# Four weight-load buffers instead of two, and two PSUM tiles for the scaling rows after attention

## The chip, the cores and the metric

The kernel runs on all eight cores of one Trainium2 chip. Each core computes one of the eight batch entries of x and has its own copy of all weights; the cores exchange nothing. The metric is the device time of the slowest core in microseconds (us). One execution of the program before was taken with the hardware profiler; the trace has all eight cores, and rows are of core 3, the slowest, where no other core is named.

## What is computed

One layer: a layer norm, differential attention with rotary embedding (two softmaxes, their weighted difference under a third softmax), a per-head RMS norm, the output projection, and beside it a feed-forward branch with Hadamard transforms, 8-bit activations and ternary weights. Cut to the lines that the two changed stages compute:

```python
def weight_quant(w):                    # for w_up and w_down
    scale = jnp.clip(jnp.mean(jnp.abs(w)), 1e-05, None)
    q = jnp.clip(jnp.round(w / scale), -1.0, 1.0) * scale
    return w + jax.lax.stop_gradient(q - w)
...
att = jnp.einsum('bhqv,bvhd->bqhd', diff, v)
att = att * jax.lax.rsqrt(jnp.mean(att * att, axis=-1, keepdims=True) + EPS) * rms_w
att = att * (1.0 - LAM_INIT)
return att.reshape(b, s, E) @ Wo
...
xn = _layernorm(x, axis=-1)
s = attention(xn)
g = _silu(hbitlinear(relu(hbitlinear(xn, w_up))**2, w_down))
x = x + s * g
```

## The kernel before

A core works through its stages one after the other: constants and the lambda row; the mean absolute value of both feed-forward weights (the weight-scale stage, from 14 us); layer norm; Hadamard transform and quantization of x; the projections to q, k and v with rotary embedding; attention (from about 2150 us); the scaling stage (5966 to 6213 us); the output projection; the two feed-forward products with a second Hadamard transform between them.

Each stage is a list of `Step`s, each with an engine, an amount by which it raises that engine's semaphore (its lane: sy for SyncE, te for TensorE, ve for VectorE, sc for ScalarE, gd for GpSimd), and an `after`: the steps it waits for. Without an `after`, a step waits for the step before it in the list. `Ch.run` (L84) emits the steps of each engine in the order of the list, inside one block, and a block ends with a barrier over all engines (the branches of L123 and L152 in the rows). A step waits at L136 until its predecessors' lanes have reached their counts. A step on SyncE or GpSimd for which another step waits also waits for its own transfer before its engine goes on (L151):

```python
if s.eng in ("sync", "gpsimd") and i in waited:
    eng.wait_ge(mysem, post[i][1])
```

So each of these two queues has at most one such transfer under way. SyncE (SP) and GpSimd (POOL) issue DMAs; VectorE is DVE, ScalarE is ACT, TensorE is PE in the rows.

The weight-scale stage (L269 to L320) goes over 64 tiles of 128 x 2048 f32 (1 MB each): 32 of the transposed up weight, 32 of the transposed down weight. Even tiles are loaded by SP, odd ones by POOL (L288), into `wst[i % 2]`, and DVE sums the absolute values of each tile into a column of `acc` (L294). The load of tile i waits for the sum of tile i-2, which is step 2 * (i - 2) + 1 of the list. Then a few small steps turn the columns into two scales.

The scaling stage (L1002 to L1026) multiplies the attention output `attT` (128 partitions, 16 heads of 2048 tokens side by side, bf16) by one factor for each head and token. The 64 rows of factors, 512 wide, lie on 64 partitions of `taub`. Each of 32 rounds brings two of them into the one-partition tile `taurow` by a 4 KB DMA on SP (L1011); then, for each of the two, an f32 matmul with a row of ones (`onr`) copies it to all partitions in the PSUM tile `psRp` (L1017, two passes of the array), and DVE multiplies a 128 x 512 piece of `attT` by it (L1022). `psRp` is another name of `psRo`; `psAt`, the PSUM tile of the attention product, is idle here. No step has an `after`, so each waits for the one before.

Of the kernel before, what the change touches and what calls it, by code (L numbers as in the profile page):

```python
# [8 lines left out]
F32 = mybir.dt.float32  # L9
# [5 lines left out]
T = 2048  # L15
# [140 lines left out]
def build_program(taps=(), upto=99):  # L156
# [29 lines left out]
    out = dt("out", [T, E], F32, "ExternalOutput")  # L186
# [13 lines left out]
    with st:  # L200
# [24 lines left out]
        onr = sbuf("onr", [1, 128], F32)  # L225
# [5 lines left out]
        with ExitStack() as ph:  # L231
            sb = lambda n, sh, ty: ph.enter_context(nc.sbuf_tensor(n, sh, ty))
# [11 lines left out]
            steps = [Step("sync", 16 * len(loads),  # L244
                          lambda e, inc, _l=loads: [inc(e.dma_start(out=d[:, :], in_=s[:, :]), 16)
                                                    for d, s in _l])]
# [22 lines left out]
        with ExitStack() as ph:  # L269
            sb = lambda n, sh, ty: ph.enter_context(nc.sbuf_tensor(n, sh, ty))  # L270
            pt = lambda n, sh: ph.enter_context(nc.psum_tensor(n, sh, F32))
            wst = [sb(f"wst{i}", [128, 2048], F32) for i in range(2)]
            acc = sb("acc", [128, 64], F32)
            ucol, dcol = sb("ucol", [128, 1], F32), sb("dcol", [128, 1], F32)
            rtmp = sb("rtmp", [1, 1], F32)
            pA, pC = pt("pA", [128, 1]), pt("pC", [128, 1])
            tiles = [(wupT, r, c) for r in range(16) for c in range(2)] + \
                    [(wdnT, r, 0) for r in range(32)]
            steps = []
            ld_idx = {}  # L280
    
            for i, (w, r, c) in enumerate(tiles):
                eng = "sync" if i % 2 == 0 else "gpsimd"
                prev_red = 2 * (i - 2) + 1 if i >= 2 else -1
                ld_idx[i] = len(steps)
                steps.append(Step(eng, 16,
                                  lambda e, inc, _w=w, _r=r, _c=c, _i=i:
                                  inc(e.dma_start(out=wst[_i % 2][:, :],  # L288
                                                  in_=_w[_r * 128:(_r + 1) * 128,
                                                         _c * 2048:(_c + 1) * 2048]), 16),  # L290
                                  after=[prev_red] if prev_red >= 0 else -1))
                steps.append(Step("vector", 1,
                                  lambda e, inc, _i=i:
                                  inc(e.reduce_sum(acc[:, _i:_i + 1], wst[_i % 2][:, :],  # L294
                                                   axis=AX, apply_absolute_value=True)),
                                  after=[ld_idx[i]]))
            for name, lo, hi, col, wsx, rws in [("u", 0, 32, ucol, wsu_s, rwsu),
                                                ("d", 32, 64, dcol, wsd_s, rwsd)]:
                steps += [
                    Step("vector", 1, lambda e, inc, _lo=lo, _hi=hi, _col=col:  # L300
                         inc(e.reduce_sum(_col[:, :], acc[:, _lo:_hi], axis=AX))),
                    Step("tensor", 1, lambda e, inc, _col=col:
                         inc(e.matmul(pA[0:1, :], onc[:, :], _col[:, :], start=True, stop=True))),
                    Step("vector", 1, lambda e, inc, _w=wsx:
                         inc(e.tensor_scalar(_w[:, :], pA[0:1, :], 1.0 / NW_ELEM, 1e-5,
                                             AO.mult, AO.max))),
                    Step("vector", 1, lambda e, inc, _w=wsx:
                         inc(e.reciprocal(rtmp[:, :], _w[:, :]))),
                    Step("tensor", 1, lambda e, inc:
                         inc(e.matmul(pC[:, :], onr[:, :], rtmp[:, :], start=True, stop=True))),  # L310
                    Step("scalar", 1, lambda e, inc, _r=rws:
                         inc(e.copy(out=_r[:, :], in_=pC[:, :]))),
                ]
            steps.append(Step("vector", 1, lambda e, inc: (
                vsync(e, e.tensor_mul(combo[:, :], wsu_s[:, :], wsu_s[:, :])),
                vsync(e, e.tensor_mul(combo[:, :], combo[:, :], wsd_s[:, :])),
                inc(e.tensor_scalar_mul(combo[:, :], combo[:, :], float(C0))))))
            ch.run(steps)
# [3 lines left out]
        with ExitStack() as ph:  # L322
            sb = lambda n, sh, ty: ph.enter_context(nc.sbuf_tensor(n, sh, ty))
# [12 lines left out]
            steps = []  # L336
# [10 lines left out]
            for tt in range(16):  # L347
                p = tt % 2
                i_ld = add1(Step("sync", 16, lambda e, inc, _tt=tt, _p=p:
                            inc(e.dma_start(out=xt[_p][:, :],  # L350
                                            in_=x[_tt * 128:(_tt + 1) * 128, :]), 16),
                            after=[pv_v2[p]]))
# [3 lines left out]
                            after=[i_ld, pv_v1[p]]))  # L356
# [6 lines left out]
                    after=[i_sq]))  # L363
# [4 lines left out]
                            after=[i_v1]))  # L368
# [6 lines left out]
                    after=[i_sr, pv_tpl[p]]))  # L375
                pv_v2[p] = i_v2
                i_c = -1
                for fp in range(8):
# [7 lines left out]
                        after=[i_v2, pv_c[fq]]))  # L386
# [3 lines left out]
                                   in_=psT[2 * _q + 1][:, :]))),  # L390
                        after=[i_t] + ([pv_st[p]] if fp == 0 else [])))
# [4 lines left out]
                                out=xnT_h.rearrange("p (f t) -> p f t", f=16)[  # L396
                                    :, :, _tt * 128:(_tt + 1) * 128],
                                in_=xstg[_p][:, :].rearrange("p (f c) -> p f c", f=16)), 16),
                            after=[i_c]))
# [5 lines left out]
        with ExitStack() as ph:  # L405
            sb = lambda n, sh, ty: ph.enter_context(nc.sbuf_tensor(n, sh, ty))
# [54 lines left out]
            steps = []  # L461
# [12 lines left out]
            for tc in range(4):  # L474
# [3 lines left out]
                for f in range(16):  # L478
# [3 lines left out]
                                                     in_=xnT_h[:, _f * T + _tc * 512:  # L482
                                                               _f * T + (_tc + 1) * 512]), 16),
                                     after=[pv_xl[r4]]))
                    i_mm = add2(Step("tensor", 1, lambda e, inc, _r=r4:
                                     inc(e.matmul(psH2[_r][:, :], h128b_s[:, :], xsl[_r][:, :],
                                                  start=True, stop=True)),
                                     after=[i_xl, pv_mm[r4]]))
# [3 lines left out]
                                     after=[i_mm] + ([pv_q[bk]] if f == 0 else [])))  # L492
# [3 lines left out]
                                 lambda e, inc, _base=base, _bk=bk:  # L496
                                 slot_store.__setitem__(_bk, butterflies(e, inc, _base, _bk)),
                                 after=[i_ev_last, pv_tree[bk]]))
                i_prev = i_bf
                for r in range(7):  # L500
                    p2 = 64 >> r
                    i_d = add2(Step("sync", 16, lambda e, inc, _p=p2, _bk=bk:
                                    inc(e.dma_start(out=ptmp[_bk][0:_p, :],
                                                    in_=mx[_bk][_p:2 * _p, :]), 16),
                                    after=[i_prev]))
# [3 lines left out]
                                       after=[i_d]))  # L509
# [4 lines left out]
                                   after=[i_prev]))  # L514
# [40 lines left out]
        with ExitStack() as ph:  # L555
# [22 lines left out]
            steps = []  # L578
# [137 lines left out]
        with ExitStack() as ph:  # L716
# [66 lines left out]
            for g in range(KVH):  # L783
                gp_ = g % 2
                for hl in range(4):
# [27 lines left out]
                    for qc in range(4):  # L813
# [192 lines left out]
                Step("vector", 1, lambda e, inc:  # L1006
                     inc(e.reciprocal(taub[0:64, :], taub[0:64, :]))),
            ]
            for sb8 in range(32):
                steps.append(Step("sync", 16, lambda e, inc, _s=sb8:  # L1010
                                  inc(e.dma_start(  # L1011
                                      out=taurow[0:1, :].rearrange("p (r c) -> p r c", r=2),
                                      in_=taub[2 * _s:2 * _s + 2, :]), 16)))
                for rr in range(2):
                    r = sb8 * 2 + rr
                    steps.append(Step("tensor", 1, lambda e, inc, _rr=rr:
                                      inc(e.matmul(psRp[:, :], onr[:, :],  # L1017
                                                   taurow[0:1, _rr * 512:(_rr + 1) * 512],
                                                   start=True, stop=True))))
                    h, qc = r // 4, r % 4  # L1020
                    steps.append(Step("vector", 1, lambda e, inc, _h=h, _qc=qc:
                                      inc(e.tensor_mul(  # L1022
                                          attT[:, _h * T + _qc * 512: _h * T + (_qc + 1) * 512],
                                          attT[:, _h * T + _qc * 512: _h * T + (_qc + 1) * 512],
                                          psRp[:, :]))))
            ch.run(steps)  # L1026
            if att_t is not None:
                ch.run([Step("gpsimd", 16, lambda e, inc:
# [454 lines left out]
```

How the kernel before makes its waits and increments, by code:

```python
                def body(eng, _e=ename):  # L125
                    for i, s in enumerate(steps):
                        if s.eng != _e:
                            continue
                        preds = _preds(i, s)
                        if preds:
                            tg = {}
                            for j in preds:
                                ln, c = post[j]
                                tg[ln] = max(tg.get(ln, 0), c)
                            for ln, c in tg.items():
                                eng.wait_ge(self.sems[ln], c)
                        else:
                            for ln, c in base.items():
                                if c > 0:
                                    eng.wait_ge(self.sems[ln], c)
                        mysem = self.sems[s._lane]
                        got = {"n": 0}
                        def inc(instr, k=1, _g=got, _s=mysem):
                            _g["n"] += k
                            return instr.then_inc(_s, k)
                        s.fn(eng, inc)
                        assert got["n"] == s.inc, \
                            f"step {i} ({s.eng}): declared inc {s.inc} != emitted {got['n']}"
                        if s.eng in ("sync", "gpsimd") and i in waited:
                            eng.wait_ge(mysem, post[i][1])
# [54 lines left out]
        def vsync(e, instr):  # L206
            instr.then_inc(vssem, 1)
            vs_n[0] += 1
            e.wait_ge(vssem, vs_n[0])
            return instr
```

## Time and profile before

| | us |
|---|---|
| timed runs, median of 2 | 9626.44 (9611.37 to 9641.5) |
| the profiled execution | 9568.67 |
| its span (slowest core, core 3) | 9567.1 |
| spans of all cores | 9525.7 to 9567.1 |
| weight-scale stage, loads and sums | 14.6 to 287 |
| scaling stage | 5966 to 6213 |

The span runs from the first to the last instruction of a core; the profiled execution's time is that of the whole run. Busy times of an engine leave out waits. A DMA issue is seen on its queue (SPq, or the POOL engine), and what its landing releases is the next instruction that used the tile. An idle time in brackets stands before the instruction, with what ended it.

### The profile page before, as it was taken

Reading aid. Unit: us, or ns where it says so; the run is one execution under the profiler, and the core shown is the slowest. Engines: PE = TensorE matmul, PEld = TensorE weight load, DVE = VectorE, ACT = ScalarE, POOL = GpSimd, SP = SyncE. Lnnn points to the kernel's source line nnn. Section 1 sums busy time; section 2 is a strip of 40 time slices with the busy share of each in tenths; the row PEclk is TensorE's granted clock in tenths of the full one; section 3 lists DMA queues with packets and bytes.
Section 4 is the critical chain, followed back from the end, with each engine's and each line's share of the span. In section 5 each row is a group of like instructions: output and inputs, shape, how many; then the busy total and the mean of one; then the engine's idle time right before and its main releaser. Section 6 shows DMA issues by size and latency. Waiting matters only on the chain. (4 is left out here: it accounts for less than half of the span.)

```text
span 9567.1 us, 61516 instructions; the slowest of 8 cores (9525.7 to 9567.1 us)
## 1 busy us (share of the span) xinstructions
PE 3498.9 (37%) x12334; PEld 1342.0 (14%) x12334; DVE 3218.8 (34%) x8586; ACT 2035.6 (21%) x5222; POOL 959.3 (10%) x1684
## 2 busy tenths in 40 slices
PE   0110256662222222222222223555677101014776
PEld 0000022220000000000000000122233101011222
DVE  5356223333333333333323333100111666672222
ACT  0310023333333333333333333000122100000111
POOL 0000444330000000000000000033011000001111
PEclk9999978885555555555555555577788555556778
DMA  6411443330000000000000000022332110102332
GB/s 234 147 34 37 79 75 77 75 59 21 15 19 16 16 17 17 21 15 15 15 21 15 15 15 10 2 34 34 128 104 88 36 30 25 36 18 66 89 86 77
DMA packets 622473, 462.03 MB, mean 48 GB/s; under 512 B 366329, under 2 KB 572394, under 8 KB 611362
## 3 DMA queue, kind: packets, MB, share of 16 engines
q1 hardware_dynamic: 437538, 269.24, 10.2%
q0 software_dynamic: 184576, 188.85, 8.8%
q8 instruction: 121, 1.98, 0.1%
q14 instruction: 238, 1.95, 0.1%
HBM read 350.52 MB, written 98.57 MB: 47 GB/s over the span
## 5 line engine op out<-in xcount | busy, mean ns | idle before, releaser
L925 PE MATMUL psT<-idn_s,Pb 128*128 128x128 bf16 x1024 | 267.8, 265 | 2027.1 <-DVE Pb L902 1897.2
L1378 PE MATMUL psD<-K,tsl 128*128 128x512 bf16 x2048 | 567.1, 446 | 87.2 <-DVE tsl L1355 87.1
L1132 PE MATMUL psU<-xqs,tsl 128*128 128x512 bf16 x2048 | 522.5, 423 | 177.4 <-DVE tsl L1122 177.4
L1055 POOL DMA_DIRECT2D wost<-wo x256 | 135.9, 602 | 4103.4 <-DVEq L123 4065.3
L891 ACT ACTIVATE Pf<-e0b 128x128 bf16<-128x128 bf16 (+15 forms) x256 | 284.0, 1109 | 855.8 <-DVE e0b L887 855.8
L687 PE MATMUL psP<-xns,wqst 128*128 128x512 bf16 x2048 | 445.7, 380 | 2.0 <-ACT vstg L663 0.3
L855 ACT ACTIVATE e0b<-psE 128x512 bf16<-128x512 f32 (+3 forms) x640 | 341.6, 534 | 409.5 <-DVE psE L850 254.3
L925 PEld LDWEIGHTS psT<-idn_s,Pb 128*128 128x128 bf16 x1024 | 107.2, 105 | 2284.6 <-issue 2271.5
L832 PE MATMUL psE<-kg,qh 128*128 128x512 bf16 (+3 forms) x640 | 326.0, 510 | 269.5 <-DMA qh<-qT_h 150.7
L963 PE MATMUL psAt<-PT,vg 128*128 128x512 bf16 x640 | 256.3, 578 | 361.9 <-DMA PT<-Pb 361.9
L701 DVE TENSOR_TENSOR m1b<-Xc,ctab 128x512 f32<-128x512 f32 x160 | 110.7, 692 | 795.0 <-ACT Xs L697 795.0
L848 DVE TENSOR_TENSOR psE<-psE,tri_s 128x128 f32<-128x128 f32 x256 | 76.5, 299 | 823.2 <-PE psE L836 823.2
L836 PE MATMUL psE<-kg,qh 128*128 128x512 bf16 (+3 forms) x640 | 341.5, 536 | 0.0
L858 ACT ACTIVATE e1b<-psE 128x512 bf16<-128x512 f32 (+3 forms) x640 | 339.3, 530 | 0.0
L1178 DVE TENSOR_TENSOR W2f<-W2f 128x256 f32<-128x256 f32 x640 | 218.1, 416 | 291.8 <-ACT W2f L1236 288.5
L1236 ACT COPY W2f<-psH 128x256 f32<-128x256 f32 x256 | 95.2, 373 | 1012.4 <-PE psH L1231 1000.1
L687 PE MATMUL psP<-xns,wkst 128*128 128x512 bf16 x512 | 121.0, 397 | 494.9 <-DMA wqst<-wq 494.9
L1265 PE MATMUL psR<-mrow,onr 1*128 1x256 f32 x16 | 9.5, 694 | 790.1 <-DVE betar L1260 790.1
L1132 PEld LDWEIGHTS psU<-xqs,tsl 128*128 128x128 bf16 x2048 | 215.6, 106 | 484.3 <-issue 294.5
L1378 PEld LDWEIGHTS psD<-K,tsl 128*128 128x128 bf16 x2048 | 224.0, 112 | 405.9 <-issue 245.0
L611 POOL DMA_DIRECT2D wqst<-wq x512 | 272.4, 987 | 14.0 <-issue 14.0
L934 ACT COPY PT<-psT 128x128 bf16<-128x128 bf16 x512 | 136.5, 267 | 599.6 <-PE psT L925 599.6
(179 smaller groups left out, 6289.0 us busy)
## 6 DMA issues: line engine op xcount, KB each, us to landing
xns<-xnT_h SPq DMA_DIRECT2D x256, 128.0 KB
wstg<-wupT SPq DMA_DIRECT2D x512, 64.0 KB
h_h<-h2b POOLq DMA_DIRECT2D x128, 256.0 KB, 2.3
W2f<-h_h SPq DMA_DIRECT2D x256, 128.0 KB
wst<-wdnT SPq DMA_DIRECT2D x512, 64.0 KB
PT<-Pb SPq DMA_TRANSPOSE x1152
wst<-wupT SPq DMA_DIRECT2D x16, 1024.0 KB
wst<-wupT POOLq DMA_DIRECT2D x16, 1024.0 KB, 5.5
```

The lines of the kernel that those rows point to most:

```text
L611: inc(e.dma_start(out=wqst[_p][:, (hl * 2 + c2) * 2048 + ec * 128: (hl * 2 + c2) * 2048 + (ec + 1) * 128], in_=wq[ec * 128:(ec + 1) * 128, ...
L687: mm = e.matmul(psP[_b][:, :], _w[:, _wc + ec * 128: _wc + (ec + 1) * 128], xns[_xp][:, ec * 512:(ec + 1) * 512], start=(ec == 0), stop=(e ...
L832: e.matmul(psE0[_b][:, 0:_cw], qh[_hp][:, _qt * 128:(_qt + 1) * 128], kg[_gp][:, _kc * 512:_kc * 512 + _cw], start=True, stop=True)
L836: inc(e.matmul(psE1[_b][:, 0:_cw], qh[_hp][:, T + _qt * 128: T + (_qt + 1) * 128], kg[_gp][:, T + _kc * 512: T + _kc * 512 + _cw], start=T ...
L855: e.activation(e0b[:, _p * T + _kc * 512: _p * T + _kc * 512 + _cw], psE0[_b][:, 0:_cw], AF.Exp, scale=ISQ, accum_out=A0[:, _p * 4 + _kc:_ ...
L858: inc(e.activation(e1b[:, _p * T + _kc * 512: _p * T + _kc * 512 + _cw], psE1[_b][:, 0:_cw], AF.Exp, scale=ISQ, accum_out=A1[:, _p * 4 + _ ...
L891: inc(e.activation(Pf[:, 0:_ks], e0b[:, _p * T: _p * T + _ks], AF.Exp, accum_out=SZ[:, _p:_p + 1]))
L925: inc(e.transpose(psT4[_tb][:, :], Pb[:, _sl * T + _kt * 128: _sl * T + (_kt + 1) * 128], idn_s[:, :])),
L963: mm = e.matmul(psAt[:, :], vg[_gp][:, kt * 128:(kt + 1) * 128], PT[:, _of + kt * 512: _of + (kt + 1) * 512], start=(kt == 0), stop=(kt == ...
L1132: mm = e.matmul(psU[_b][:, :], tsl[_p][:, ec * 128:(ec + 1) * 128], xqs[:, ec * T + _tc * 512: ec * T + (_tc + 1) * 512], start=(ec == 0), ...
L1178: last = e.tensor_sub(W[free[idx]][:, :], W[slot[i]][:, :], W[slot[j]][:, :])
L1378: mm = e.matmul(psD[_b][:, :], tsl2[_p][:, ec * 128:(ec + 1) * 128], K2[:, ec * T + _tc * 512: ec * T + (_tc + 1) * 512], start=(ec == 0), ...
```

## The change

In the weight-scale stage there are four buffers `wst` (their tiles are now called wstt) and tile i goes to buffer i % 4; its load waits for the sum of tile i-4. In the scaling stage each step has an explicit `after`. The two rows of a round go to two PSUM tiles, `psRp` and `psAt`. A matmul waits for its round's DMA and for the multiply that last read its tile; a multiply waits for its matmul; and the DMA of a round waits for the second matmul of the round before.

```diff
-            wst = [sb(f"wst{i}", [128, 2048], F32) for i in range(2)]
+            wst = [sb(f"wstt{i}", [128, 2048], F32) for i in range(4)]
...
-                prev_red = 2 * (i - 2) + 1 if i >= 2 else -1
+                prev_red = 2 * (i - 4) + 1 if i >= 4 else -1
...
-                                  inc(e.dma_start(out=wst[_i % 2][:, :],
+                                  inc(e.dma_start(out=wst[_i % 4][:, :],
...
-                                  inc(e.reduce_sum(acc[:, _i:_i + 1], wst[_i % 2][:, :],
+                                  inc(e.reduce_sum(acc[:, _i:_i + 1], wst[_i % 4][:, :],
...
+            ps45 = [psRp, psAt]
+            pv_mul = {0: -1, 1: -1}
+            pv_mm2 = [-1]
             for sb8 in range(32):
-                steps.append(Step("sync", 16, lambda e, inc, _s=sb8:
+                i_d = add45(Step("sync", 16, lambda e, inc, _s=sb8:
...
+                                 after=[pv_mm2[0]] if sb8 else [1]))
                 for rr in range(2):
                     r = sb8 * 2 + rr
-                    steps.append(Step("tensor", 1, lambda e, inc, _rr=rr:
-                                      inc(e.matmul(psRp[:, :], onr[:, :],
+                    i_mm = add45(Step("tensor", 1, lambda e, inc, _rr=rr:
+                                      inc(e.matmul(ps45[_rr][:, :], onr[:, :],
...
+                                      after=[i_d, pv_mul[rr]]))
...
+                                       after=[i_mm]))
+                    pv_mul[rr] = i_mul
+                pv_mm2[0] = i_mm
```

What SP issues at the start of the weight-scale stage, before the change (the number behind wst is the buffer, L_sy, L_ve, L_te and L_sc are the lanes waited for, and x15 stands for fifteen such issues):

```order
L245 DMA oh_s<-ohd 128x127
L123 UNCONDITIONAL_BRANCH [waits L_sy]
L152 UNCONDITIONAL_BRANCH [waits barrier_Pool_Activation_PE_DVE_SP_release]
L288 DMA wst0<-wupT 128x2048 [waits L_sy,L_ve,L_te,L_sc]
L288 DMA wst0<-wupT 128x2048 [waits L_sy,L_ve] x15
L288 DMA wst0<-wdnT 128x2048 [waits L_sy,L_ve] x16
```

The same place of SP after the change:

```order
L152 UNCONDITIONAL_BRANCH [waits barrier_Pool_Activation_PE_DVE_SP_release]
L288 DMA wstt0<-wupT 128x2048 [waits L_sy,L_ve,L_te,L_sc]
L288 DMA wstt2<-wupT 128x2048 [waits L_sy,L_ve,L_te,L_sc]
L288 DMA wstt0<-wupT 128x2048 [waits L_sy,L_ve]
L288 DMA wstt2<-wupT 128x2048 [waits L_sy,L_ve]
L288 DMA wstt0<-wupT 128x2048 [waits L_sy,L_ve]
```

SP now alternates between buffers 0 and 2 (POOL between 1 and 3). Every issue still waits for the own lane L_sy, that is for SP's load before it; the wait for DVE is for an older sum.

What stands on TensorE at the start of the scaling stage before the change (each row is a matmul of two passes):

```order
L152 UNCONDITIONAL_BRANCH [waits barrier_Pool_Activation_PE_DVE_SP_release]
L1017 MATMUL psRo<-taurow,onr 128x512 [waits L_sy]
L1017 MATMUL psRo<-taurow,onr 128x512 [waits L_ve]
L1017 MATMUL psRo<-taurow,onr 128x512 [waits L_sy]
L1017 MATMUL psRo<-taurow,onr 128x512 [waits L_ve]
```

And after the change:

```order
L152 UNCONDITIONAL_BRANCH [waits barrier_Pool_Activation_PE_DVE_SP_release]
L1026 MATMUL psRo<-taurow,onr 128x512 [waits L_sy]
L1026 MATMUL psAt<-taurow,onr 128x512 [waits L_sy]
L1026 MATMUL psRo<-taurow,onr 128x512 [waits L_sy,L_ve]
L1026 MATMUL psAt<-taurow,onr 128x512 [waits L_sy,L_ve]
```

The order of the matmuls is the same; the second of a round now has its own PSUM tile and waits for the DMA rather than for the multiply just before it. On SP the DMA of a round waits for TensorE's lane instead of VectorE's. Before:

```order
L983 DMA msb<-msrow 1x16x32 [waits L_sy,L_sc]
L123 UNCONDITIONAL_BRANCH [waits L_sy]
L152 UNCONDITIONAL_BRANCH [waits barrier_Pool_Activation_PE_DVE_SP_release]
L1011 DMA taurow<-taub 1x2x512 [waits L_ve]
L1011 DMA taurow<-taub 1x2x512 [waits L_sy,L_ve] x31
```

And after:

```order
L983 DMA msb<-msrow 1x16x32 [waits L_sy,L_sc]
L123 UNCONDITIONAL_BRANCH [waits L_sy]
L152 UNCONDITIONAL_BRANCH [waits barrier_Pool_Activation_PE_DVE_SP_release]
L1019 DMA taurow<-taub 1x2x512 [waits L_ve]
L1019 DMA taurow<-taub 1x2x512 [waits L_sy,L_te] x31
```

Nothing is added to or taken from any queue, and nothing changes its place in one.

## Rows read from the trace of the kernel before

**Rows 1.** The page: the span, and the chain that ended last, by engine.

```profile
span 9567.1 us, 61516 instructions; the slowest of 8 cores (9525.7 to 9567.1 us)
...
PE 6%; DVE 1%; ACT 1%; issue 1%; SPq 0%; DMA 0%; DVEq 0%; ACTq 0%; POOLq 0%; POOL 0%
```

**Rows 2.** Busy time by stretch: the two stages. Columns as in the first row.

```profile
core 3: us, PE busy (x) PEld busy (x) DVE busy (x) ACT busy (x) POOL busy (x), PEclk, DMA share, GB/s
14.00:285.00 271.00, 0.00 (x0) 0.00 (x0) 144.06 (x64) 0.14 (x1) 17.08 (x32) 1.00 0.73 248
5966.00:6215.00 249.00, 130.62 (x128) 31.72 (x128) 44.18 (x65) 0.00 (x0) 1.44 (x3) 0.50 0.00 1
```

**Rows 3.** One tile: SP's loads to wst, durations in ns, first and last start.

```profile
L288 SPq DMA_DIRECT2D wst<-wupT x16: 327/328/328, 14.6 to 138.4; - x16
...
L288 SPq DMA_DIRECT2D wst<-wdnT x16: 327/328/328, 147.6 to 274.6; - x16
```

**Rows 4.** SP's own waits, 14 to 290 us: total, times, longest.

```profile
SPq L151 <- DMA wst<-wdnT: 90.5, 16, 7.6
SPq L151 <- DMA wst<-wupT: 88.0, 16, 6.0
SPq L136 <- DVE acc L294: 73.0, 31, 2.4
```

**Rows 5.** In order of time, one turn of POOL's loop: start, length, what.

```profile
84.53 0.53 POOL L288 DMA_DIRECT2D wst<-wupT  x1 [8.02 <-DVE acc L294]
...
89.84 2.29 DVE L294 TENSOR_REDUCE acc<-wst 128x1 f32<-128x2048 f32 x1 [2.00 <-DMA wst<-wupT]
92.68 0.53 POOL L288 DMA_DIRECT2D wst<-wupT  x1 [7.62 <-DVE acc L294]
```

**Rows 6.** One line: SP's DMAs of the scaling stage.

```profile
L1011 SPq DMA_DIRECT2D taurow<-taub x32: 558/558/621, 5966.3 to 6204.9; - x32
```

**Rows 7.** In order of time: the first round of the scaling stage.

```profile
5966.30 46.78 SPq L1011 DMA_DIRECT2D taurow<-taub  x7
...
5968.15 2.04 PE L1017 MATMUL psRo<-taurow,onr 1*128 1x512 f32 x2 [10.17 <-DMA taurow<-taub]
5970.30 0.69 DVE L1022 TENSOR_TENSOR attT<-attT,psRo 128x512 bf16<-128x512 bf16 x1 [4.08 <-PE psRo L1017]
...
5971.14 2.04 PE L1017 MATMUL psRo<-taurow,onr 1*128 1x512 f32 x2 [0.94 <-DVE attT L1022]
5973.28 0.69 DVE L1022 TENSOR_TENSOR attT<-attT,psRo 128x512 bf16<-128x512 bf16 x1 [2.29 <-PE psRo L1017]
```

**Rows 8.** Busy time in 17 to 22.5 us: cores 3, 5 and 0.

```profile
17.00:22.50 5.50, 0.00 (x0) 0.00 (x0) 2.29 (x1) 0.00 (x0) 0.00 (x0) 1.00 0.89 326
...
17.00:22.50 5.50, 0.00 (x0) 0.00 (x0) 0.80 (x1) 0.00 (x0) 0.00 (x0) 1.00 0.95 237
...
17.00:22.50 5.50, 0.00 (x0) 0.00 (x0) 1.93 (x1) 0.00 (x0) 0.00 (x0) 1.00 1.01 264
```

**Rows 9.** Busy time and granted clock: bursts of bf16 (L1065) and f32 matmuls (L1231).

```profile
6214.00:6224.00 10.00, 0.05 (x1) 0.08 (x2) 0.00 (x0) 0.00 (x0) 8.05 (x16) 0.50 0.57 53
6224.00:6229.00 5.00, 5.00 (x14) 1.79 (x15) 0.00 (x0) 0.00 (x0) 0.00 (x0) 0.55 0.00 0
6229.00:6234.00 5.00, 5.00 (x25) 2.29 (x24) 0.00 (x0) 2.46 (x3) 0.56 (x1) 1.00 0.09 30
...
7431.00:7434.00 3.00, 2.94 (x7) 2.43 (x8) 0.00 (x0) 1.66 (x3) 0.00 (x0) 0.50 0.00 0
7437.00:7440.00 3.00, 3.00 (x15) 2.64 (x14) 0.00 (x0) 2.42 (x7) 0.00 (x0) 1.00 0.00 0
```

**Rows 10.** In order of time: the first two loads on core 0, then core 3.

```profile
14.88 43.84 SPq L288 DMA_DIRECT2D wst<-wupT  x6
15.43 0.68 POOL L288 DMA_DIRECT2D wst<-wupT  x1 [14.74 <-POOLq L123]
...
25.27 2.29 DVE L294 TENSOR_REDUCE acc<-wst 128x1 f32<-128x2048 f32 x1 [2.41 <-DMA wst<-wupT]
...
14.63 98.61 SPq L288 DMA_DIRECT2D wst<-wupT  x13
...
22.95 2.29 DVE L294 TENSOR_REDUCE acc<-wst 128x1 f32<-128x2048 f32 x1 [0.95 <-DMA wst<-wupT]
```

More of the change, by code:

```diff
@@ L1008, in build_program, with add45 @@
             ]
-            for sb8 in range(32):
-                steps.append(Step("sync", 16, lambda e, inc, _s=sb8:
-                                  inc(e.dma_start(
-                                      out=taurow[0:1, :].rearrange("p (r c) -> p r c", r=2),
-                                      in_=taub[2 * _s:2 * _s + 2, :]), 16)))
+            def add45(stp):
+                steps.append(stp)
+                return len(steps) - 1
+            ps45 = [psRp, psAt]
+            pv_mul = {0: -1, 1: -1}
@@ L1014, in build_program @@
+            pv_mm2 = [-1]
+            for sb8 in range(32):
+                i_d = add45(Step("sync", 16, lambda e, inc, _s=sb8:
+                                 inc(e.dma_start(
+                                     out=taurow[0:1, :].rearrange("p (r c) -> p r c", r=2),
+                                     in_=taub[2 * _s:2 * _s + 2, :]), 16),
+                                 after=[pv_mm2[0]] if sb8 else [1]))
                 for rr in range(2):
                     r = sb8 * 2 + rr
-                    steps.append(Step("tensor", 1, lambda e, inc, _rr=rr:
-                                      inc(e.matmul(psRp[:, :], onr[:, :],
+                    i_mm = add45(Step("tensor", 1, lambda e, inc, _rr=rr:
+                                      inc(e.matmul(ps45[_rr][:, :], onr[:, :],
@@ L1018, in build_program @@
                                                    taurow[0:1, _rr * 512:(_rr + 1) * 512],
-                                                   start=True, stop=True))))
+                                                   start=True, stop=True)),
+                                      after=[i_d, pv_mul[rr]]))
                     h, qc = r // 4, r % 4
[L1021 to L1025, printed above, removed]
+                    i_mul = add45(Step("vector", 1, lambda e, inc, _h=h, _qc=qc, _rr=rr:
+                                       inc(e.tensor_mul(
+                                           attT[:, _h * T + _qc * 512: _h * T + (_qc + 1) * 512],
+                                           attT[:, _h * T + _qc * 512: _h * T + (_qc + 1) * 512],
+                                           ps45[_rr][:, :])),
+                                       after=[i_mm]))
```

## The prediction, made before the changed kernel ran

> **What bounds the kernel now.** I read the page first. Its chain of waits ends in the last matmul stage and covers some 8% of the span [rows 1]; the change touches nothing there. So the question is what two early stages are worth, each closed off by a barrier on both sides, so that whatever they gain moves the end by the same amount. I then took the stretches of the two stages, the counts and first and last starts of their instructions, SP's own waits, and one turn of each loop in order of time.
>
> The weight-scale stage: in 14 to 285 us the core does nothing but load 64 tiles of 1 MB and sum them. DVE is busy 144 of 271 us, the DMA share is 0.73 at 248 GB/s [rows 2]. SP's 32 loads start from 14.6 to 274.6 us, so a turn of SP's loop (two tiles, since POOL loads the other) is 260.0/31 = 8.39 us [rows 3]. SP's waits split it: 88.0 + 90.5 us over 32 for its own transfer (5.58 us each) and 73.0 over 31 for the reduce (2.35) [rows 4]; with 0.33 for the issue that is 8.26, and the rest hand-over. The reader should see one thing here: the queue issues one load, waits for it (L151), and only then for the reduce, so that each queue has at most one load in flight. On POOL the turn is issue 84.53, reduce from 89.84 (5.31 later), its end 2.29 later, next issue at 92.68, 0.55 after that [rows 5].
>
> The scaling stage after attention: 32 rounds that hold one small DMA, two f32 matmuls and two DVE multiplies. In 5966 to 6215 us PE is busy 52%, DVE 18%, and nothing else runs [rows 2]. SP issues from 5966.3 to 6204.9: 238.6/31 = 7.70 us a round [rows 6]. A round in order of time, counted from its DMA issue at 5966.30: matmul at 1.85, 2.04 long; multiply at 4.00, 0.69 long; second matmul at 4.84 (0.94 idle before it, released by DVE); second multiply at 6.98, done at 7.67; next DMA at 7.70 [rows 7]. Everything stands on one string.
>
> **The change in the load stage.** With four buffers the load i waits for reduce i-4, not i-2. It does not put more loads in flight: L151 still holds each queue until its own load has landed. What goes is the 2.35 us for the reduce from SP's turn, and 2.29 from POOL's. What is late next is the landing itself. If it stayed as it is, SP's turn would be 5.58 + 0.33 + about 0.1 = 6.0 us and POOL's 5.31 + 0.55 = 5.9. But 2.10 MB in 6.0 us is 350 GB/s, against 248 now, so landings may stretch. Bounds from rows: at the present ratio of rate to DMA share, a full share would be 248/0.73 = 340 GB/s, 6.2 us a turn. The only stretch of before with both queues loading at once on all cores is the start: in 17 to 22.5 us core 3 moves 326 GB/s at share 0.89 and core 5 237 GB/s at 0.95 [rows 8], which would be 6.4 and 8.8 us a turn; core 0 moves 264, 7.9 us. These first windows hold the ramp of the first transfers, so I lean to the fast side and take 6.6 us (318 GB/s), nearest to core 3, the core of this profile. Gain 31 x (8.39 - 6.6) = 55 us; ends 31 x (8.39 - 6.0) = 74 and 31 x (8.39 - 7.9) = 15, core 5's figure being left to the rivals. DVE hides under it: two reduces are 4.57 us plus some 0.2 between. The buffers cost nothing else; they are freed with the stage. POOL's later DMAs keep their place.
>
> [...]
>
> **The change in the scaling stage.** The two rows now go to two PSUM tiles, each matmul waits only for the DMA and for the multiply of the round before on its own tile, and the DMA waits for the second matmul in place of the second multiply. All instructions stay (32 DMAs, 64 matmuls of two passes, 64 multiplies). The round becomes: DMA to first matmul 1.85; four passes of f32 in a row; hand-over from PE to SP, about 0.1 (PE to DVE is 0.11 in the rows); next DMA. The four passes: two end after 2.04, and the second starts some 0.99 after the first, so two more add between 1.71 (twice 0.427 x 2, from the f32 passes of half the width, 7 in 3.0 us at the same clock [rows 9]) and 2.04. I take 1.90, so 3.94 in all, and a round of 1.85 + 3.94 + 0.1 = 5.89. The first multiply (0.69) lies beside the second matmul, the second beside the next DMA: it starts about 0.1 after the second matmul and is done some 1 us before the next round's first matmul, so the new waits on DVE are met long before. Behind a waiting matmul nothing is queued but the other matmul of the round. Gain 31 x (7.70 - 5.89) + 1.0 for the last round, whose first multiply is now hidden, = 57 us; ends 52 (four full passes, hand-over 0.15) and 63 (3.75 and 0.05).
>
> **Sum.** 55 + 57 = 112 us. The profiled execution took 9568.7 us, its span 9567.1; it would become 9456. The timed runs' median, 9626.4, is 58 above it, for reasons no row shows; I carry the gain over unchanged: 9626 - 112 = 9514 us. That is 1.2%, while a measurement of this kernel can tell about 2% from no change; so the sum, even if exactly right, counts as "within 2%".
>
> **Rivals.**
> Memory-bound: the loads already run at what memory gives to eight cores, and landings stretch as fast as the wait for the reduce goes. For it: share 0.73 now, and core 5 and core 0 at share 0.95 or more with 237 and 264 GB/s at the start. Against it: core 3's 326 GB/s at the same time. It would give 0 to 20 us, say 10: 9626 - 10 - 57 = 9559.
>
> [...] In the new order bursts are 3.9 us and gaps 2.0. The clock rose in rows only within longer unbroken bursts: 0.50 just before 6224, 0.55 in the first 5 us of a burst and 1.00 after that; there 14 matmuls in 5 us become 25, and the f32 passes go from 7 to 15 in 3 us [rows 9]. [...] If it rose, the four passes would take about 2.0 us; over two thirds of the rounds that is 21 x 1.9 = 40 us more: 9474. [...]
>
> Slower: with both queues of all eight cores always loading, the transfers trip over each other, as in the first pair. On core 0 that pair's second load, issued at 15.43, was reduced only at 25.27, and the first one was issued at 14.88: 10.4 us for two tiles [rows 10]. If every turn took that, the stage would lose 31 x (10.4 - 8.39) = 62 us and eat the 57 of the other: 9631, slower than before. It decides from a turn of 8.39 + 57/31 = 10.2 us on. Against it: the turn fell to 8.39 once loads were staggered, and core 3's first pair needed 8.3 us (14.63 to 22.95), start-up included [rows 10].
>
> Not as said: the second PSUM tile is no real second place, or the DMA still waits for DVE. The order of instructions shows neither; it would leave the gain of loads, 9571.
>
> **How the numbers follow.** Forecast 0.58, memory-bound 0.20, clock rises 0.13, slower than before 0.04, not as said 0.05. The likeliest is 9514. The range takes in memory-bound (9559, with some 25 us of scatter, as the two timed runs lie 30 apart) and the clock (9474, less the 19 us by which the load stage could beat its term): 9455 to 9585. Faster by over 2% needs 193 us, that is the clock over all rounds (60), both terms at their good ends (74 + 63): 197; chance 0.04. Slower by over 2% needs a turn of 16 us: 0.01. Within 2%: 0.95.
>
> **What would show it.** Right: SP's 32 weight loads from 14.6 to about 14.6 + 31 x 6.6 = 219 us, SP's waits for the reduce near zero and those for its landing above 5.6 us each, share over 0.9, DVE idle still released by DMA; in the scaling stage a round of 5.9 us, PE's idle time before the first matmul about 2 us and before the second none, SP released by PE. All other stages keep their lengths. Wrong: a turn above 7.5 us (memory-bound), above 10.2 (slower); a granted clock over 0.50 after attention (clock); 0.9 us idle still before every second matmul (not as said); or a later stage that changes by over 10 us, for which I name no cause.

## The result

Over all runs the changed kernel took 9504.65 us (median of 11, 9455.8 to 9589.55) and the kernel before 9625.29 (median of 10, 9547.24 to 9658.55). The ratio is 0.9882 with a 95% interval of 0.9843 to 0.992, so the change takes off 77 to 151 us, 114 in the middle: it is faster, by less than 2%. The forecast was 112 us and a time of 9514. Ratios compare fast executions alone, since in some executions of five of the kernels here cores 0 to 3 or cores 4 to 7 show a lower granted clock and take over 1% longer, as in one of the kernel before: cores 0 to 3 took 9705.2 to 9765.2 us at 0.661 to 0.665, the others 9523.1 to 9573.0 us at 0.678 to 0.683.

The profiled execution of the changed kernel took 9536.69 us; its slowest core is now core 4. Core 3, the core of the rows of before, went from 9567.1 to 9464.1. The first line of the page of the changed kernel, against [rows 1]:

```profile
span 9534.6 us, 61584 instructions; the slowest of 8 cores (9443.3 to 9534.6 us)
```

From the view of all cores, spans and mean granted clock of three; the other five end between 9443.3 and 9473.1, so cores 4 and 5 stand apart, of which more in the last section:

```profile
core 3: 9464.1 us, clock 0.677
core 4: 9534.6 us, clock 0.677
core 5: 9499.9 us, clock 0.682
```

The load stage of the changed kernel on core 3: SP's loads with their first and last start, against [rows 3].

```profile
L288 SPq DMA_DIRECT2D wstt<-wupT x16: 327/328/331, 14.8 to 125.0; - x16
...
L288 SPq DMA_DIRECT2D wstt<-wdnT x16: 327/328/328, 132.4 to 241.2; - x16
```

SP's waits there, against [rows 4]:

```profile
SPq L151 <- DMA wstt<-wupT: 109.9, 16, 8.1
SPq L151 <- DMA wstt<-wdnT: 108.4, 16, 7.7
```

The wait for the reduce (73.0 us before) has no row any more. SP's turn is (241.2 - 14.8)/31 = 7.30 us, against 8.39. But the landing, 5.58 us of waiting a load before, is now (109.9 + 108.4)/32 = 6.82: of the 2.35 us of waiting that went, 1.24 came back as a longer landing. The busy times of the stage and of the scaling stage on core 3, against [rows 2]:

```profile
core 3: us, PE busy (x) PEld busy (x) DVE busy (x) ACT busy (x) POOL busy (x), PEclk, DMA share, GB/s
14.00:251.00 237.00, 0.02 (x1) 0.00 (x0) 143.91 (x63) 0.17 (x1) 17.09 (x32) 1.00 0.87 283
5919.00:6097.00 178.00, 115.90 (x124) 35.92 (x124) 42.20 (x62) 0.00 (x0) 0.00 (x0) 0.50 0.00 1
```

One round of the scaling stage in order of time, against [rows 7]:

```profile
5919.38 6.26 SPq L1019 DMA_DIRECT2D taurow<-taub  x2
...
5921.23 2.04 PE L1026 MATMUL psRo<-taurow,onr 1*128 1x512 f32 x2 [10.17 <-DMA taurow<-taub]
...
5923.06 1.91 PE L1026 MATMUL psAt<-taurow,onr 1*128 1x512 f32 x2
...
5923.37 0.69 DVE L1032 TENSOR_TENSOR attT<-attT,psRo 128x512 bf16<-128x512 bf16 x1 [4.08 <-PE psRo L1026]
5925.08 0.69 DVE L1032 TENSOR_TENSOR attT<-attT,psAt 128x512 bf16<-128x512 bf16 x1 [1.02 <-PE psAt L1026]
5926.94 0.49 PEld L1026 LDWEIGHTS psRo<-taurow,onr 1*128 1x128 f32 x2 [3.54 <-issue]
5926.97 2.04 PE L1026 MATMUL psRo<-taurow,onr 1*128 1x512 f32 x2 [2.00 <-DMA taurow<-taub]
```

The second matmul has no idle time before it, where it had 0.94 us; the four passes take from 5921.23 to 5924.97, 3.74 us; the next matmul waits 2.00 us for its DMA. From first to last DMA it is 5919.4 to 6097.3, so a round is 5.74 us against 7.70, and this was the same on all eight cores. On core 3 the stages gave 33.8 us (the last sum of the load stage ends at 253.4, not 287.2) and 61.8 (31 rounds of 1.96 and the shorter last round). That is 96 of its 103 us. The rest is scatter of the other stages: between the last sum and the first multiply of the scaling stage core 3 took 5683 us before and 5670 after, while the cores of the kernel before take 5651 to 5691 there; and behind the scaling stage it lost 6 us.

### The profile page after: what moved, and what is told of

Read it like the earlier page. It is cut to its first block and busy times, and to the rows that moved or that the text cites. A ratio compares the mean times of both kernels' runs of the same rounds, so it can differ in the third digit from the quotient of the medians.

```text
span 9534.6 us, 61584 instructions; the slowest of 8 cores (9443.3 to 9534.6 us)
## 1 busy us (share of the span) xinstructions
PE 3489.5 (37%) x12334; PEld 1348.3 (14%) x12334; DVE 3221.7 (34%) x8586; ACT 2036.2 (21%) x5222; POOL 961.6 (10%) x1684
## 5 line engine op out<-in xcount | busy, mean ns | idle before, releaser
L1244 PE MATMUL psH<-W2f,h128f_s 128*128 128x256 f32 x512 | 133.7, 430 | 359.4 <-DMA W2f<-h_h 359.4
```

## The experiments

All but two are told against the changed kernel; lines of each are those of core 3.

**The loads alone.** The first three hunks of the change, the scaling stage as before.

> Four load buffers, the scaling stage as before the change. Theory (the two gains are independent, each stage closed off by barriers): SP's turn in the load stage 7.3 to 7.4 us as in the changed kernel, so 33 to 39 us off the time; the scaling stage keeps its 7.70 us a round. Rival (the load stage only shifts the cores against each other and a later stage gives the gain back): the same turn, but the layer norm to attention stretch longer by 20 us or more, time within 10 us of before.

It took 9598.41 us against 9636.99 of before, ratio 0.9958 (0.9921 to 0.9994): 40 us, between 6 and 76. SP's turn was 7.11 to 7.25 us over the cores, a little under the expected 7.3, and the round 7.70. The interval of the time alone does not exclude the rival of a later stage that gives the gain back, but the stage lengths do: from the last sum to the scaling stage the cores took 5657 to 5696 us, before 5651 to 5691. Cores 2 and 3 did lose 46 to 49 us in one later stage, which comes back in the last section.

**The scaling stage alone.**

> Two load buffers as before, the scaling stage as changed. Theory: SP's turn in the load stage back at 8.4 to 8.7 us, a scaling round of 5.74 us as in the changed kernel, 62 us off the time. Rival (the scaling stage gains more because it is reached earlier, at another granted clock): a round clearly other than 5.74 us, or a granted clock over 0.50 in it.

9561.18 us, ratio 0.9925 (0.9885 to 0.9964): 72 us, between 35 and 111. The turn was 8.32 to 8.61 us, the round 5.74, the granted clock 0.50. That the two parts are independent is shown by the turn and the round: each part alone has the value of the whole change in its own stage and that of before in the other. The times agree, 40 + 72 = 112 against 114, but each is uncertain by over 30 us.

**More loads in flight.** This asks what holds the turn at 7.3 us: memory, or the one load for each queue.

```diff
-                        if s.eng in ("sync", "gpsimd") and i in waited:
+                        if s.eng in ("sync", "gpsimd") and i in waited and not s._lane.startswith("wl"):
...
-                                  after=[prev_red] if prev_red >= 0 else -1))
+                                  after=[prev_red] if prev_red >= 0 else -1,
+                                  lane=f"wl{i % 4}"))
```

> As the changed kernel, but each of the four load buffers has its own semaphore and the queues no longer wait for their own load before they issue the next, so that up to four loads are in flight. Theory memory-bound (eight cores together get no more than the 283 GB/s per core seen in the changed kernel): the mean rate stays at 275 to 300 GB/s, two tiles every 7.0 to 7.6 us, 0 to 10 us gained in the stage. Rival, one load per queue is the bound (start-up of each load is exposed): rate 340 GB/s or more, two tiles in at most 6.2 us, 35 us or more gained.

**One queue.** SP issues all 64 loads: `eng = "sync"` for every tile.

> As the changed kernel, but SP issues all 64 loads, each after the one before has landed: one load in flight in a core. It prices a load without the core's other queue. If landings of the changed kernel (6.8 us on SP) are stretched by sharing, a lone load lands after 5.0 to 5.4 us, and the stage takes 64 x 5.6 = 358 us, 125 us more than in the changed kernel. If a load takes its 6.8 us on its own, sharing costs nothing and the stage takes 64 x 7.2 = 460 us.

The two kernels took 9446.94 and 9552.68 us, one execution each. The stretch 50 to 200 us lies within the load stage in all kernels, so one row of each gives a scale from one load in flight to four. In this order: the kernel with one queue, before, changed, more in flight (columns as in [rows 2]).

```profile
50.00:200.00 150.00, 0.00 (x0) 0.00 (x0) 67.11 (x31) 0.00 (x0) 0.00 (x0) 1.00 0.62 209
```

```profile
50.00:200.00 150.00, 0.00 (x0) 0.00 (x0) 80.33 (x36) 0.00 (x0) 9.51 (x18) 1.00 0.73 249
```

```profile
50.00:200.00 150.00, 0.00 (x0) 0.00 (x0) 94.16 (x42) 0.00 (x0) 10.57 (x20) 1.00 0.86 286
```

```profile
50.00:200.00 150.00, 0.00 (x0) 0.00 (x0) 105.16 (x47) 0.00 (x0) 12.48 (x24) 1.00 0.99 325
```

One load at a time gives 209 GB/s, two that wait for their reduce 249, two without that wait 286, four 325 with the DMA share at 0.99 (over the eight cores 205 to 209, 245 to 250, 283 to 293 and 316 to 330). So 286 was not yet what can be had, and the memory-bound theory falls at the number it named. Its rival named 340 GB/s, a turn of at most 6.2 us and 35 us gained; the runs gave 325, 6.46 and 23 us on core 3 (last sum at 230.0, not 253.4), so it was right in kind and too high in size. The rate divided by the share is 337, 341, 333 and 328 GB/s in these rows (over the eight cores 333 to 357, 335 to 345, 316 to 334 and 317 to 331): nearly constant, so a load that lands later does so mainly because more loads share the core's 16 DMA engines, and less because its packets take longer. The packet records of core 3 agree: from 60 to 180 us no packet at all was under way for 33 us with one load at a time, for 13 before, for 3 after the change and for none with four. The waits of SP in the kernel with one queue:

```profile
SPq L151 <- DMA wstt<-wupT: 149.9, 32, 5.5
SPq L151 <- DMA wstt<-wdnT: 144.1, 32, 4.8
```

A load with nothing beside it in its core is waited for 294.0/64 = 4.59 us, below the 5.0 to 5.4 expected, and the last sum ends at 340.9 us, 87 us later than in the changed kernel and not 125. With the other queue stopping for its reduces the wait is 5.58, with it always loading 6.82. With four in flight the median from issue to landing was 10.1 us, which costs nothing, because no queue stands still for its own load: SP's turn was (215.3 - 15.0)/31 = 6.46 us, and the wait is for DVE again, as this row of SP's waits there shows.

```profile
SPq L136 <- DVE acc L295: 188.0, 30, 9.5
```

That row names DVE, but a sum is late only since its tile is: DVE is busy 105 of 150 us in this stretch.

**The second PSUM tile alone.** The DMA waits for the second multiply again.

```diff
-                                 after=[pv_mm2[0]] if sb8 else [1]))
+                                 after=[pv_mul[1]] if sb8 else [1]))
```

> As the changed kernel, but the DMA of a round waits for the second multiply again: only the second PSUM tile is left of the edit of the scaling stage. Theory: the 0.94 us between the first matmul and the second go (a little more, if the passes follow closer), the multiply before the DMA comes back: a round of 6.6 to 6.75 us. Rival (the second PSUM tile brings nothing without the earlier DMA, or the two parts need each other): 7.70 us a round.

**The early DMA alone.** One PSUM tile, each matmul behind the multiply before it.

```diff
-            ps45 = [psRp, psAt]
+            ps45 = [psRp, psRp]
...
-                                      after=[i_d, pv_mul[rr]]))
+                                      after=[i_d, pv_mul[1 - rr]]))
```

> As the changed kernel, but both rows of a round go to one PSUM tile and each matmul waits for the multiply before it; the DMA still waits for the second matmul only. Theory: the 0.83 us from the end of the second matmul to the DMA shrink to about 0.1: a round of 6.85 to 7.0 us. Rival (the DMA hides nothing, the multiply is then in front of the next matmul): 7.70 us.

The rounds were 6.53 us with the PSUM tile alone and 7.01 with the early DMA alone, each just outside the range expected and far from the 7.70 of its rival. The gains are 1.17 and 0.69 us of 7.70; together 1.86, and the whole change has 1.96. The two rows that tell it, the first of the kernel with the PSUM tile alone, the second of the kernel with the early DMA:

```profile
5938.33 1.19 PE L1026 MATMUL psRo<-taurow,onr 1*128 1x512 f32 x1 [2.79 <-DMA taurow<-taub]
```

```profile
5953.40 2.04 PE L1026 MATMUL psRo<-taurow,onr 1*128 1x512 f32 x2 [0.94 <-DVE attT L1032]
```

Each keeps just the wait that it did not address: 2.79 us for the DMA instead of 2.00, and 0.94 for DVE. The times of both kernels, 9541.45 and 9649.01 us in one execution each, tell little, the second above all: see the last section.

**Two row tiles.** The DMA of a round is issued two rounds behind the matmuls that last read its tile.

```diff
-            taurow = sb("taurow", [1, 2 * 512], F32)
+            taurow = [sb(f"taurow{i}", [1, 2 * 512], F32) for i in range(2)]
...
-                                 after=[pv_mm2[0]] if sb8 else [1]))
+                                 after=[pv_mm2[-2]] if sb8 >= 2 else [1]))
...
-                pv_mm2[0] = i_mm
+                pv_mm2.append(i_mm)
```

> As the changed kernel, with two row tiles, so that the DMA of a round is under way while the matmuls of the round before run. [...] Rival (an unbroken burst raises the clock, as with the matmuls of L1065 and L1231 before the change): clock 1.00 from some 5 us into the stage on, a round of about 2 to 2.6 us, then bound by the DMA's 1.85 us and its hand-over, stage about 70 to 85 us.

SP's DMAs run from 5917.1 to 6021.7. The second is issued right behind the first; from the third on they come every 3.41 us, which is four passes of 0.853 us and nothing else, on all cores the same and faster than the 3.6 to 3.9 that I had taken for a round of the four passes alone. From the first DMA to the last multiply the stage takes 112 us, against 184 in the changed kernel and 246 before. The kernel's one execution took 9396.79 us. The busy times of the stage:

```profile
5922.00:5927.00 5.00, 5.00 (x7) 1.73 (x7) 2.06 (x3) 0.00 (x0) 0.00 (x0) 0.50 0.00 1
5927.00:6020.00 93.00, 93.00 (x110) 33.77 (x110) 37.12 (x54) 0.00 (x0) 0.00 (x0) 0.50 0.00 2
```

TensorE is busy in every one of 98 us, and the granted clock stays at 0.50. So the rival on the clock falls here, and with a far denser burst than the changed kernel's.

**Both, as a faster version.** Four loads in flight and two row tiles.

> The load stage with up to four loads in flight together with the scaling stage with two row tiles. [...]

9405.98 us, ratio to before 0.9788 (0.9751 to 0.9825): 204 us off, against 114 of the change. By stages, on core 3 it has 28 us less than the changed kernel in the load stage and 72 less in the scaling stage. I had expected to come out some 60 us under the changed kernel if the load rate stayed at its 283 GB/s and the granted clock at 0.50, and some 140 if both rose; it is 100 by the stages, since the rate rose, to 331 GB/s in 50 to 200 us on core 3, and the clock stayed at 0.50 through the burst on all cores. Its slowest of six executions (9426.97) is faster than the fastest of the changed kernel (9455.8), so it beats both kernels; whether by over 2% against before, the interval leaves open.

**A selector instead of the row DMAs.** DVE writes a one-hot selector of 64 x 128 for each row, and the matmul over 64 partitions picks the row out of `taub`, with no DMA left in the stage.

```diff
-                                      inc(e.matmul(ps45[_rr][:, :], onr[:, :],
-                                                   taurow[0:1, _rr * 512:(_rr + 1) * 512],
-                                                   start=True, stop=True)),
-                                      after=[i_d, pv_mul[rr]]))
+                                    inc(e.matmul(ps45[_rr][:, :],
+                                                 sqb[0:64, (_r % 4) * 128:(_r % 4 + 1) * 128],
+                                                 taub[0:64, :], start=True, stop=True)),
+                                    after=[1, sels[r], pv_mul[rr]]))
```

> As the changed kernel, but the scaling stage has no row DMAs: each row of factors is copied to all partitions by an f32 matmul over 64 partitions of taub, against a one-hot selector that DVE writes for each row. With two row tiles and one-row matmuls TensorE ran unbroken for over 100 us at a granted clock of 0.50. Theory (how many rows of the array are active decides, since the f32 matmuls over 128 rows of L1231 did raise the clock): the clock goes to 1.00 within some 6 us, two passes take 0.85 us, and DVE bounds the stage with 64 x (0.69 + 0.2 to 0.3) plus gaps, about 65 to 80 us. Rival (the clock stays low for any matmul in this stage): 0.50 throughout, 64 x 1.71 = 109 us as with two row tiles.

> Up to four loads in flight in the load stage, with the scaling stage of the selector kernel. SP's turn 6.3 to 6.5 us as with more in flight; the scaling stage as in the selector kernel. By the theory of active rows some 30 us less than the kernel with four loads in flight and two row tiles (9406 us), about 9375 us; by the rival about the same as it.

The clock stayed at 0.50 through this stage too, on all cores, and the matmuls took the 109 us that the rival gives (first to last start 6014.4 to 6122.9): the theory fell for 64 rows. The profiled execution took 9480.02 us, and its stage on core 3 starts late because cores 2 and 3 spent some 100 us more than the others between the load stage and attention. The combination with four loads in flight took 9430.6 us, ratio 0.9808 (0.9764 to 0.9852), no better than with two row tiles, as the rival had it.

**Dense weights over 64 and over 128 rows.** The selector is replaced by the Hadamard matrix `h128f_s`: its first 64 rows against `taub[0:64, :]`, then all 128 rows against `sqb`. Both multiply attT by other numbers than the factors.

> The scaling stage of the selector kernel with the Hadamard matrix's first 64 rows (all entries plus or minus 1) as weights in place of the one-hot selector, so that attT is multiplied by other numbers than the factors; same instructions on TensorE, same shapes. Theory (weights that are nearly all zero leave the array idle in the eyes of the clock): the clock goes to 1.00 within 6 us, a matmul takes 0.85 us and DVE's 0.69 plus hand-over bounds the stage near 55 to 60 us. Rival (the number of active rows decides, 64 are too few, or f32 at this width never does it): 0.50 throughout, 64 x 1.71 = 109 us.

> As the kernel with 64 dense rows, but over all 128 rows: the whole Hadamard matrix against sqb, the squares left by the last attention tile; attT is multiplied by other numbers. If dense weights decide: as with 64 dense rows. If active rows decide: clock 1.00 within 6 us here, and 0.50 with 64. If both kernels stay at 0.50 for 109 us, neither rows nor weights are what the matmuls of L1231 had, and the clock's cause stays open.

With 64 rows, 5918 to 6020 us in two stretches:

```profile
5918.00:5923.00 5.00, 5.00 (x7) 1.77 (x6) 2.06 (x3) 0.00 (x0) 0.00 (x0) 0.50 0.00 0
5923.00:6020.00 97.00, 97.00 (x114) 35.18 (x114) 39.02 (x57) 0.00 (x0) 0.00 (x0) 0.50 0.00 0
```

With 128 rows, from 5905 us:

```profile
5905.00:5910.00 5.00, 4.00 (x5) 1.80 (x6) 1.87 (x5) 0.00 (x0) 0.00 (x0) 0.50 0.00 0
5910.00:5915.00 5.00, 4.92 (x9) 1.60 (x8) 2.72 (x5) 0.00 (x0) 0.00 (x0) 0.78 0.00 0
5915.00:5970.00 55.00, 52.84 (x109) 16.06 (x108) 37.09 (x55) 0.00 (x0) 0.00 (x0) 1.00 0.00 0
```

With 64 active rows the weights make no difference: one-hot and dense alike stay at a granted clock of 0.50, on all cores. With all 128 rows the granted clock on core 3 goes to 1.00 some 6 us into the burst, and from the first matmul to the last multiply the stage takes 69 us, not 110. Five more cores did the same (68 to 69 us), but cores 4 and 5 lost part of the clock again, down to 0.81, without a pause in the burst, and took 74 and 72 us. Core 4, whose burst began at 5968.9:

```profile
5988.00:6040.00 52.00, 51.92 (x94) 15.78 (x92) 31.84 (x47) 0.00 (x0) 0.00 (x0) 0.81 0.00 0
```

The run with 128 rows differs from that with 64 in its moving data as well (`sqb`, the squares, in place of `taub`, the factors), so rows and data are not told apart by these two runs alone. At a granted clock of 1.00 DVE is busy 37 of 55 us and is not the bound: a PSUM tile goes round in 2.04 us, made of 1.20 from the start of a matmul to its multiply, 0.69 for the multiply and 0.15 to the next matmul, and there are two tiles. The rows of one round of `psAt` on core 3:

```profile
5915.72 1.10 PE L1033 MATMUL psAt<-sqb,h128f_s 128*128 128x512 f32 x2
...
5916.92 0.69 DVE L1038 TENSOR_TENSOR attT<-attT,psAt 128x512 bf16<-128x512 bf16 x1 [0.49 <-PE psAt L1033]
...
5917.76 1.10 PE L1033 MATMUL psAt<-sqb,h128f_s 128*128 128x512 f32 x2
```

The profiled executions of the two kernels took 9445.39 and 9407.41 us.

## Why the prediction was right

The bound was read rightly: both stages were strings of waits closed off by barriers, each part gave in its own stage what the whole change gives there, and the gains add. The rest goes by its steps.

The load stage, forecast 55 us, gave 34 on core 3 and 34 to 42 over the cores, 37 in the mean. What went and what is late next were right; the term that was mis-sized is the landing, by way of the turn: 6.6 us was taken, 7.30 measured, within the bounds of 6.0 and 7.9. I had leaned on core 3's 326 GB/s at the start, taking two queues always loading to be able to hold it. They hold 286: a queue moves nothing between a landing and the first packet of its next load, which in the kernel with one queue comes 0.94 us after the issue (median on core 3), and only four loads in flight fill that gap (DMA share 0.99 in 50 to 200 us, against 0.86). The rate of 318 that I took is near that of the kernel with more in flight. Two of the signs that I named did not come either: the last load was to start at 219 us and started at 241, and the DMA share was to be over 0.9 and was 0.86 to 0.91 over the cores. The bound from the DMA share, 248/0.73 = 340 GB/s, was good: 325 at 0.99. The highest means on core 3 in 50 to 200 us are these 325 and the 331 of the kernel with both. The second issuer gave 286 GB/s against 209 with one, since in this kernel each issuer waits for its own load; with four loads in flight and no such wait the two gave 325.

The scaling stage, forecast 57 us, gave 61.8. The round was 5.74 us, not 5.89: 1.85 to the first matmul, 3.74 for the four passes and 0.15 of hand-over to SP. The passes were taken at 3.94; they came out just under the short end of 3.75 to 4.08, because those of the second matmul follow at 0.853 us, twice the 0.427 of the passes of half the width in [rows 9]. The ends of this term, 52 and 63, were added wrongly: from the parts named for them they are 51 and 65, which changes nothing else. Each half of the edit alone removed the wait that I had read off the round for it (0.94 before the second matmul, 0.83 between it and the DMA), to within 0.25 us.

The sum of the two stages is 96 us on core 3 and 99 in the mean of the cores, 13 to 16 under the forecast of 112: the load term missed by 21 on core 3 and the scaling term by 5 the other way. The runs give 114, but with an interval of 77 to 151 that holds both. So the forecast's gain was too large by some 15%, and that it came within 2 us of the runs' middle is luck.

Of the rivals, memory-bound was the nearest in size: the landing did stretch, by half of what the wait had cost. But the cause was mostly the loads' sharing of the DMA engines, and not a limit of memory at 286 GB/s, as the 325 with four loads show. The granted clock stayed at 0.50. That the forecast holds it there was right, the reason was not: I had taken bursts of 3.9 us as shorter than those before a rise in [rows 9], but with two row tiles it stayed there through 98 us without a gap, so the burst's length was not what kept it there. The slower case's turn of 10.4 us was seen nowhere; 7.43 is the longest of the changed kernel. The case "not as said" falls with the idle time before the second matmul, which is gone. And "a later stage that changes by over 10 us, for which I name no cause" did come, on cores 4 and 5.

## What to carry to other kernels

More buffers help a queue only up to what the issuing engine lets fly: look for the wait on its own transfer, and give each buffer its own semaphore before adding buffers; here four buffers in place of two gave 34 us on core 3 with that wait, and 23 more without it. In a string of small steps read the idle time before each one and its releaser; every such row is an edit with its own price, and here two of them added up to within 0.1 us. Where eight cores run one program, compare stage lengths core by core before a difference of half a per cent is put down to an edit.

## What the runs showed of the hardware

**Two cores of a pair in step.** In the profile of the changed kernel cores 4 and 5 spend 55 to 63 us more than the others in the stage that loads the hidden layer back and transforms it (`W2f`, eight times 4 MB; its length is taken from the first load to the last matmul). TensorE's wait for these loads on core 4 and on core 3, in all, times, longest:

```profile
PE psH L1244 <- DMA W2f<-h_h: 359.4, 8, 47.7
```

```profile
PE psH L1244 <- DMA W2f<-h_h: 303.4, 8, 40.6
```

Cores 4 and 5 began it at 7322.4 and 7323.9 us, within 1.5 us of each other; cores 0 and 1 at 7299.2 and 7289.1. Each profile has four such pairs (0 and 1, 2 and 3, and so on), and over the 14 kernels, before and changed among them, the table is this:

| distance of the two starts | pairs | length of the stage |
|---|---|---|
| 0.4 to 2.3 us | 9 | 1151 to 1202 us |
| 3.8 to 6.8 us | 9 | 1127 to 1155 us |
| 8.3 us and more | 38 | 1123 to 1141 us |

All nine pairs within 2.3 us lost 24 to 75 us here, against a length of 1127, whatever the kernel. Two rows of the changed kernel, 5 us in the middle of such a load on core 3 and on core 4, show how:

```profile
7308.00:7313.00 5.00, 0.00 (x0) 0.00 (x0) 0.00 (x0) 0.00 (x0) 0.00 (x0) 0.50 0.91 275
```

```profile
7332.00:7337.00 5.00, 0.00 (x0) 0.00 (x0) 0.00 (x0) 0.00 (x0) 0.00 (x0) 0.50 0.91 193
```

The DMA engines are as busy on core 4, but move 193 GB/s and not 275: here the packets themselves take longer, and from the first issue of a load to the first matmul it takes 25 us and not 18. That the two cores contend for something they share when their loads fall together is what the rows suggest; no run sets the distance by hand, so that part is argued. It is not plain sharing of a rate, though: in pairs 7 to 16 us apart the loads of 18 us still overlap for a time, and yet they took 18.3 us each in the median, with four of 544 above 20 us (in the pairs within 2.3 us the median is 24.1). What the two cores share stays open.

In the stretch before this one, the output projection and the first product, some cores lost time too, but the distance does not tell which. Cores 0 to 3 of the kernel with the early DMA alone took 1262 to 1287 us from the last row DMA on, against 1208, and with the stage above this makes its 9649 us; their mean granted clock over the whole execution was lower as well (0.668 against 0.678). But cores 4 and 5 of the changed kernel entered this stretch 1.6 us apart and lost nothing, while cores 2 and 3 of the kernel with 64 dense rows entered it 7.3 us apart and lost over 40 us. So pairs in step are one source of the scatter between executions and not the only one. They may be part of the 58 us between the profiled execution of before, which has no pair within 2.3 us, and the median of its runs: eight of the fourteen profiles have at least one such pair, and the slowest core sets the time.

**The clock and the rows of the array.** f32 matmuls 512 wide, back to back for about 100 us, ran at a granted clock of 0.50 on all eight cores with 1 active row and with 64, dense or one-hot. With 128 rows, and other moving data, the clock rose to 1.00 some 6 us into the burst on core 3, and on cores 4 and 5 it was back at 0.81 before the burst ended. So an unbroken burst alone did not raise the clock: in the runs with two row tiles, with the selector and with 64 dense rows TensorE had no gap either. If the rows are the cause, padding the 64 rows of factors to 128 would give the scaling stage the high clock, by the run with 128 rows some 68 to 74 us instead of 110 from the first matmul on; that was not tried.
